# Layer norms of the retention layers applied on ScalarE, with the shift made on GpSimd, in place of VectorE

## What is computed

```python
for i in range(L):                                   # L = 4, D = 128, F = 256, 8 heads of 16
    Yr = _retention(_layer_norm(X, ln_scale, ln_bias), Wq[i], Wk[i], Wv[i], Wg[i], Wo[i],
                    gn_scale[i], gn_bias[i], Dm, cos, sin) + X
    X = gelu(_layer_norm(Yr, ln_scale, ln_bias) @ W1[i]) @ W2[i] + Yr

def _layer_norm(x, scale, bias):
    mu = x.mean(-1, keepdims=True)
    var = x.var(-1, keepdims=True)
    return (x - mu) * rsqrt(var + 1e-5) * scale + bias
```

## Time and profile before

| what | value |
| --- | --- |
| median of 3 runs | 904.27 us (901.36, 904.27, 2293.99) |
| span of the profiled execution | 902.2 us |
| PE busy | 694.0 us, 77% of the span |
| DVE busy | 710.4 us, 79% |
| ACT busy | 400.5 us, 44% |
| POOL busy | 540.6 us, 60% |
| mean granted clock of PE | 0.911 of full |

### The profile page before, as it was taken

How to read it: one execution, slowest core, us unless ns; L and a number is a source line. 1 busy time by engine, 2 the same in 40 slices (tenths; PEclk the granted TensorE clock), 3 DMA queues, 4 the chain that set the end, 5 groups by cost and what they waited for, 6 DMA issues and landing times. The chain is left out here.

```text
span 902.2 us, 13308 instructions
## 1 busy us (share of the span) xinstructions
PE 694.0 (77%) x4382; PEld 446.9 (50%) x4384; DVE 710.4 (79%) x1531; ACT 400.5 (44%) x594; POOL 540.6 (60%) x427
## 2 busy tenths in 40 slices
PE   3995666566576665547478999989998999978985
PEld 1442222222222222426266777757776777756764
DVE  4589999997999999674657777757775777677986
ACT  1984333432424332054465555445444444444641
POOL 5125777765767676475647667746775777753322
PEclk9998888998879989857799999989999999998998
DMA  8000000000000000000000000000000000000000
GB/s 289 0 1 0 0 0 0 0 0 0 0 0 0 0 0 1 0 0 1 1 2 1 2 19 11 13 3 19 10 12 3 19 10 12 3 0 1 13 12 24
DMA packets 7015, 10.88 MB, mean 12 GB/s; under 512 B 560, under 2 KB 5296, under 8 KB 6576
## 3 DMA queue, kind: packets, MB, share of 16 engines
q1 hardware_dynamic: 6960, 10.12, 3.4%
HBM read 9.07 MB, written 1.05 MB: 11 GB/s over the span
## 5 line engine op out<-in xcount | busy, mean ns | idle before, releaser
L533 POOL TENSOR_TENSOR arena<-arena 128x1024 f32<-128x1024 f32 x64 | 206.6, 3248 | 87.7 <-DVE arena L916 51.0
L1211 PE MATMUL psum<-arena,Cs 128*128 128x512 f32 x256 | 149.6, 717 | 104.5 <-POOL arena L533 104.5
L916 DVE TENSOR_TENSOR_SCAN arena<-arena 128x1024 f32<-128x1024 f32 x64 | 207.1, 3275 | 0.0
L682 ACT ACTIVATE arena<-arena 128x1020 f32<-128x1020 f32 x64 | 73.2, 1145 | 173.9 <-DVE arena L916 171.1
L1211 PEld LDWEIGHTS psum<-arena,Cs 128*128 128x128 f32 x256 | 53.9, 222 | 177.8 <-POOL arena L533 133.2
L472 POOL TENSOR_TENSOR ve<-mv,eps 128x4 f32<-128x4 f32 x52 | 11.2, 215 | 167.3 <-DVE mv L834 167.3
L580 POOL TENSOR_TENSOR arena<-arena,mhalf 128x32 f32<-128x32 f32 x16 | 86.8, 5426 | 2.0 <-DVE arena L1033 2.0
L750 ACT ACTIVATE arena<-arena,Cs 128x512 f32<-128x512 f32 x96 | 62.2, 713 | 48.2 <-POOL arena L575 48.2
L1146 PE MATMUL psum<-Wl,arena 128*128 128x128 f32 x512 | 72.7, 294 | 5.5 <-ACT arena L777 4.0
L1139 PE MATMUL psum<-Cs,arena 128*128 128x128 f32 x240 | 39.7, 292 | 47.0 <-ACT arena L693 23.3
L911 DVE TENSOR_TENSOR arena<-arena,psum 128x1024 f32<-128x1024 f32 x64 | 74.3, 1200 | 0.6 <-PE psum L1205 0.6
(11 more groups left out here) (162 smaller groups left out, 1360.3 us busy)
## 6 DMA issues: line engine op xcount, KB each, us to landing
Wl<-wl SPq DMA_DIRECT2D x4, 384.0 KB, 3.1
Wa<-wa SPq DMA_DIRECT2D x1, 1251.0 KB, 6.9
Wd<-wd SPq DMA_DIRECT2D x1, 1100.0 KB, 12.1
X<-x SPq DMA_DIRECT2D x4, 256.0 KB, 7.6
Sel<-sel SPq DMA_DIRECT2D x1, 1024.0 KB, 9.4
Wl<-wl SPq DMA_DIRECT2D x4, 256.0 KB, 3.3
out<-X SPq DMA_DIRECT2D x4, 256.0 KB, 2.3
Wl<-wl SPq DMA_DIRECT2D x4, 192.0 KB, 2.4
```

Of the source, the lines that this page charges most:

```text
L533: pool.tensor_tensor(Hc[:, h], Hs[:, r, h], Crows[:, r], ALU.mult).then_inc(hc_ready, 1)
L682: act.activation(Da[:, h].rearrange(seq, s=S)[:, :, 1:], Dt[:, h, cols].rearrange(seq, s=S)[:, :, 1:], ACT.Exp, scale=Aneg[:, bass.ds(pair ...
L916: dve.tensor_tensor_scan(Hs[:, r, h], Da[:, h], Dbu[:, h], 0.0, ALU.mult, ALU.add).then_inc(scanned, 1)
L1211: ins = pe.matmul(bank[2 * h + c][:], ident, Hc[:, h, group(c)], start=False, stop=False, skip_group_check=True)
```

## The change

`norm1` and `norm2` of the retention layers are no longer done by DVE but by ACT, one ACTIVATE for each tile, at the same place of the common list; POOL calls `rstd_and_shift` in place of `rstd` for them. The other norms stay where they are. ACT gets a counter (`norms`) by which it knows which value of `rstd_ready` to wait for.

```diff
-PER_LAYER_VECTOR = 2 * G * (3 * GT - 1) + 3 * G
+PER_LAYER_VECTOR = 2 * G * (2 * GT) + 3 * G
-PER_LAYER_POOL = 2 * G + 2 * G
+PER_LAYER_POOL = 2 * G * 3 + 2 * G
...
@@ POOL, layer_steps
                     if what in ("stats1", "stats2"):
-                        rstd(g)
+                        rstd_and_shift(g)
...
@@ ACT, layer_steps
+                    if what in ("stats1", "stats2", "var"):
+                        due[what, g] = norms.next()
+                    if what in ("norm1", "norm2"):
+                        act.wait_ge(rstd_ready, due.pop(("stats" + what[-1], g)))
+                        for t in range(g * GT, (g + 1) * GT):
+                            ins = act.activation(Hn3[:, t, :], R3[:, t, :], ACT.Identity, bias=shift[:, t:t + 1], scale=rs[:, t:t + 1])
+                        ins.then_inc((c_normed if what == "norm1" else f_normed).sem, 1)
                     if what == "turn1":
                         act.wait_ge(*c_turned.at(layer, g))
...
@@ DVE, layer_steps
                     if what == "norm1":
-                        normalise(Hn3, R3, g, c_normed.sem)
+                        due.pop(g)
...
                     if what == "norm2":
-                        normalise(Hn3, R3, g, f_normed.sem)
+                        due.pop(g)
```

More of the change, by code:

```diff
@@ L623, in _ @@
             own = Steps(act, act_steps)
+            norms = Counter()
+            due = {}
             act.wait_ge(wa_in, 16)
@@ L778, in layer_steps @@
                                            ACT.Gelu_apprx_tanh).then_inc(gelu_ready.sem, 1)
+            for _ in range(G):
+                norms.next()
             for step in OPENING:
                 if step[0] in TREE_STEPS:
+                    if step[0] in ("t1", "g_stats", "b_stats", "t2_stats", "rx_stats"):
+                        norms.next()
                     tree_step(step[0], step[2])
@@ L786, in _ @@
             with act.Fori(0, LAYERS - 1) as layer:
+                assert not [k for k in due if k[0] != "var"]
+                due.clear()
                 own.enter(layer, PER_LAYER_SCALAR)
+                norms.enter(layer, 3 * G)
                 layer_steps(LAYER, layer)
                 own.leave(LAYERS - 1)
+                norms.leave(LAYERS - 1)
             one = (0, 0)
@@ L794, in _ @@
                 what, part, g, _ = step
+                if what in ("r_stats", "x_stats", "t_stats"):
+                    norms.next()
                 if what not in EXPERT_STEPS:
```

## The result

The changed kernel takes 944.17 us (median; 940.77 to 949.60), the kernel before 902.82 us with the runs beside it: a ratio of 1.0469, with a 95% interval of 1.0425 to 1.0513. It is slower by 4.7%. One of the four runs of the kernel before took 2293.99 us; the ratio leaves it out. The profiled execution has a span of 944.1 us, 41.9 us more than before, at a mean granted clock of 0.909 (0.911 before).

What follows compares the result with a forecast made beforehand. It took PE's list to bound the ring: ring 12 x 2.1 = 25, opening 6.4, ending 1 and clock 11 made +43 us on a span of 902.2, forecasting 946 us, with 930 to 961 for 8 times in 10.

Steps and rivals of the forecast that it cites:

- What bounds the ring, and the slack: In the ring, the loop with the changed norms, PE's list sets the time; `norm1` has 0.2 us of slack before `turn1`.
- The main term: `norm1` waits behind the copies of `values` on ACT, so PE pauses 2.1 us at `turn1` in each slot.
- What is queued behind it: In a slot, `norm2` and the tanh of `gate` behind it on ACT stay hidden, as PE is 2.1 us later too.
- Opening: The four slots before the loop: delays at `turn1` of 0.9, 1.9, 1.5 and 2.1 us, together 6.4 us.
- Ending: After the loop: three `norm2`, small delays against DVE's relief, taken as +1 us between bounds of -3 and +3.
- The clock: PE's clock falls after some of the 15 pauses of about 2 us, adding 11 us.
- The half: For PE's clock, half of the 22.5 us between never falling and falling after each pause was taken: +11 us.
- The price per fall: Each fall of PE's clock behind a pause costs 1.5 us.
- The upper bound: PE's clock falls after each of 15 pauses, +22.5 us; a rival with this or a second wait gave 957 us, chance 0.14.
- The one without a wait behind `values`: Rival: on ACT `norm1` runs ahead of `values`, PE's pause at `turn1` is 0.7 us, 915 us in all; chance 0.07.
- DVE as the bound: Rival: DVE bounds the kernel after all, its 35 us of norms come off, giving 867 us; chance 0.03.
- The signs: In the traces: 15 idle times of about 2.1 us at `turn1`, released by ACT; turn 97 to 100 us; clock below 0.98.

Runs made afterwards that it cites:

- run 8: Changed kernel with `norm1` ahead of `values` in ACT's order, and `gate` ahead of `turn1` and `norm2` in the common list: 907.24 us, ratio 1.0038.
- run 3: Kernel before with `rstd_and_shift` on POOL for both norms, the shift unused, all norms still on DVE: 910.10 us, ratio 1.0077.
- run 4: Changed kernel with `norm1` moved ahead of the two copies of `values` in ACT's order: 912.91 us, ratio 1.0117.
- run 1: Kernel before with only `norm1` moved to ACT, `norm2` left on DVE: 942.44 us, ratio 1.0438.
- Run 2: Kernel before with only `norm2` moved to ACT, `norm1` left on DVE: 917.14 us, ratio 1.0165.
- run 7: Kernel before with only `norm2` moved to ACT, placed behind the tanh of `gate` in ACT's order: 905.99 us, ratio 1.0026.
- Run 5: Changed kernel with two 128x512 matmuls added on PE in front of each `turn1`: 925.66 us, ratio 1.0237.
- run 9: Changed kernel with two matmuls only 8 columns wide added on PE in front of each `turn1`: 934.61 us, ratio 1.0336.
- run 12: The kernel of run 8 with two 8-column matmuls added in front of `turn1` in the opening alone: 898.09 us, ratio 0.9941.

## Why the prediction was right

*What bounds the ring, and the slack.* Right. PE's list sets the time: taking 29 us of work off DVE brought nothing (run 8), and 0.42 us more on POOL were felt at once (run 3). The slack of 0.2 us from the earlier trace rows was real.

*The main term*, 2.1 us in each slot. Measured 1.94 us of idle time and 2.16 us per slot; the transposes, which began before `scores 1` had ended (650.56 in the earlier trace rows), now begin after it, and that is the rest. Two small readings of the chain were off and cancel: ACT's norm starts 0.03 us behind the copies and not 0.1 us inside them, and PE starts 0.04 us after the norm and not 0.14. That the place behind `values` makes it, and not the norm's length, is shown by run 4; that it is `norm1`, by run 1.

*What is queued behind it.* `norm2` and the tanh are hidden in the changed kernel, as said: PE's `rotate` starts at 682.65 without a wait. Run 2 shows the price when the cover is gone: 14 us. The prediction gave that cover a price only for `norm2`'s own arrival. The tanh behind it was the costlier part, 12 of the 14 us (run 7).

*Opening*, 6.4 us. PE's idle times at the four `turn1` grew by 0.93, 1.94, 1.56 and 1.94 us, together 6.4.

*Ending*, +1. From the last pause in the ring on, it is about 0.5 us. One piece I had not seen: in the first slot of the ending `mix` waits 2.57 us for DVE, which waits for the tanh behind `norm2`, where it waited 0.86 us. A later wait covers it.

*The clock*, +11. Seven falls in 15 pauses, at 1.65 us each (24.68 less 23.03): 11.6 us. The half was a choice between bounds which no row settled; that it came out is luck. The price per fall, 1.5 us from the earlier trace rows, was 10% low. The upper bound, a fall behind every pause, did not come. The term is also gross: the changed kernel has lost falls that the kernel before had. Its pause for POOL in the opening, 1.97 us with a fall in the earlier trace rows, is now 1.64 us, without one (timeline, and windows view of what follows):

```profile
497.82 0.66 PE L1158 MATMUL psum<-Cs,arena 128*128 128x128 f32 x4 [1.64 <-POOL arena L593]
497.80:501.20 3.40, 3.38 (x48) 2.98 (x48) 2.05 (x9) 1.34 (x3) 1.57 (x4) 1.00 0.00 0
```

With PE's instructions of both kernels lined up, the missing fall gives back about 1.5 us, and the one at the first edge of the loop, which is shorter than before, about 0.6. So the clock's net share is about 9 us and not 11.6. The prediction did not look for falls that go. Run 5 against run 9 shows that this part is caused by the pause: 9 us come back when PE has work in it. A pause of 1.94 us can thus cost the clock or not, in one and the same kernel; what decides it, no run here shows.

*Rivals.* The one without a wait behind `values` was a fair account of another kernel (915 forecast, 912.91 in run 4). DVE as the bound is refuted by runs 8 and 12. The times beside that rival, 1.65 against 1.10 us, show DVE quicker at this work; that a faster mode is the reason, no row shows.

*The signs.* A turn was to grow to about 97 to 100 us; it takes 100.5 and 101.8, a little more, since the two turns have three and two falls of the clock each. The other signs came as said.

The sum, 946 us, stands against 944.17. The terms as measured are 25.9 for the ring (12 x 2.16), 6.4 for the opening, 0.5 for the ending and about 9 for the clock, together 42 for the 41.9 by which the span grew. It was right for the reasons given, by the runs above; that it came within 2 us owes something to the chosen half. What the sum left out: the edge of the loop, 10 us of either kernel, which I took as fixed, and which has nothing to do with the change.

## What to carry to other kernels

Before moving work to an engine with idle time, look at what stands ahead of its new place in that engine's order, and what stands behind it: here ACT was idle for over half the time and the norm still waited 1.47 us for it, and the order, not the load, made three quarters of the loss. A step that has 0.2 us of slack is on the path. And when an engine waits for "issue" at the top of a loop, count its instruction fetches: where the loop's code starts can be worth 1% and costs a few idle instructions to change. A change of another kind that moves the loop's start could win or lose as much by that alone, so look at the edge of the loop before crediting the change.

## What the runs showed of the hardware

- PE's clock fell to half behind 7 of 15 nearly equal pauses (1.94 to 1.97 us), at 1.65 us of time for each fall, behind 6 of 15 of about 1.60 us with two 8-column matmuls ahead of the transposes, and behind none when two 128x512 matmuls filled them.
- With the same loop of 808 matmuls and 808 weight loads in a turn, PE's code was fetched anew in each turn (38 packets) or held for the later turns (20), by the place where it starts; the jump back cost PE 3.36 and 3.71 us of idle time or 0.17 and 0.21 us.
- Four ACTIVATEs of 128 columns with scale and bias from memory take 1.65 us together, on tiles in the arena as in X; DVE's four `tensor_scalar` 1.10 us.
